# Rotary attention: two queue positions moved, ScalarE's half-precision copy of the queries and GpSimd's subtraction for it

## The chip, the cores and the metric

The program runs on one core of one Trainium2 chip. A core has five engines that run their own instruction queues and wait for each other by semaphores: TensorE (PE in the profile, PEld its weight loads), VectorE (DVE), ScalarE (ACT), GpSimd (POOL) and SyncE (SP, which issues transfers). The metric is the time of one execution on the device in microseconds; lower is better. Before the change it is 3782.42 us (median of 3 runs, 3779.88 to 3782.56).

## The reference

The whole network has eight parts in two layers (modulation, Nystrom attention, LSTM, head-routed attention; then adapter, rotary attention, recurrent network, experts). The change touches the rotary attention of the second layer alone:

```python
q = apply_rope(q)            # t*cos + rotate_half(t)*sin
k = apply_rope(k)
k = concatenate([pm, k]); v = concatenate([pm, v])     # 4 memory rows ahead of 512 tokens
scores = einsum('bhid,bhjd->bhij', q, k) * dim_head**-0.5
scores = where(causal, scores, finfo.min)
attn = softmax(scores, axis=-1)
out = einsum('bhij,bhjd->bhid', attn, v)
return out.transpose(...) @ w_out.T
```

It runs over 8 batches of 512 tokens with 16 heads of 64. Operands are kept in two half-precision parts, a high one (the value rounded) and a low one (what the rounding left), and TensorE multiplies high by high, high by low and low by high.

## The kernel before

`attention_core` takes the heads in pairs: 8 pairs in a batch, 2 batches in a turn of the loop, so 64 slots of one pair each, with a short run-in. A slot `s` works on four pairs at once: it ends pair `s-1` (weights times values, outputs), does the scores and the exponentials of pair `s`, the plain scores and maxima of pair `s+1`, and the projection and rotation of queries and keys of pair `s+2`. Each engine has its own function `rope_slot`, which is the order of its queue written out by hand. After every 8 pairs an output projection is added ("out" slots, L1028), and once in 8 slots the tokens of a later batch are split into high and low (`low_tokens`, L1151; called a new-batch slot here).

The rotation of one 128x512 block of queries (index `q`) or keys (index `k`) goes through four engines:

- PE projects into the PSUM tile `pj` (L832).
- DVE multiplies it by the cosines (L979) and shuffles neighbours (L980) into the two halves of `ab`, which releases `pj`.
- POOL multiplies the second half by the signed sines (`turn`, L1138) and adds the halves into `rot` (`sum_up`, L1142).
- ACT copies `rot` to half precision (`high`, L1080); POOL subtracts that from `rot` and stores the low part (`low`, L1147).

`ab` and `rot` are single buffers here. So DVE's next rotation waits for the sum before it, and a sum waits for `low` of the block before it.

The other DVE work named below: L1007 subtracts the high from the full exponentials, in four pieces for four key tiles of 128x1024, 776, 520 and 264 elements (called piece 0 to 3), with a tail of 4x8 (L1010); L990 and L991 are maxima of scores; L997, L1001 and L1003 split the maxima; L1024 makes the low part of the outputs; L1019 to L1021 normalise; L1014 makes the low values. On ACT L1088 and L1093 are the two exponentials of a tile (`exps`), L1101 keeps outputs, L1083 the turned maxima and L1098 the high values.

Of the kernel before, what the change touches and what calls it, by code (L numbers as in the profile page):

```python
# [760 lines left out]
def attention_core(nc, XT, HT, c_):  # L761
# [15 lines left out]
    def slots(run,eng):  # L777

        for s in (-2,-1,0): run(0,s)
        with loop(nc,eng,NB//BPI) as it:  # L780
            for s in range(1,S+1): run(it,s)
    def first_query(t): return max(0,P*t-PM) if rope else 0
    def key_columns(qt): return P*qt+P+PM if rope else T
    def written(t): return P_AT[t]+(PAD if rope and t else 0)
# [3 lines left out]
    with ExitStack() as ctx:  # L788
# [22 lines left out]
        def sliced(X,k,it): return X[:,k,bass.ds(it,1),:].rearrange("p a t -> p (a t)")  # L811
        block=ctx.enter_context(nc.Block())
        def batch(it,n): return (it*BPI+n//NP_)%NB
        def h_of(n): return hT[:,(n//NP_)%HB]
        def rot_of(j): return rot[:,0 if rope else j%2]
# [256 lines left out]
        @block.scalar  # L1072
        def _(act):
            act.wait_ge(cleared,CL)
            def high(it,j):
                n,what=divmod(j,2)
                if what and rope: nc.scalar.activation(QK[:,n%4,1,:,0:PM],c_.pmk[:,n%NP_],ACT.Copy).then_inc(pm_kept,1)
                act.wait_ge(summed if rope else evac,it*2*S+j+1)
                dst=QK[:,n%4,1,0,PM:PM+T] if what else QK[:,n%4,0,0,0:T]
                nc.scalar.activation(dst,rot_of(j),ACT.Copy).then_inc(hi,1)  # L1080
            def keep_max(it,n):
                act.wait_ge(m_turned,it*S+n+1)
                nc.scalar.activation(mT[:,:],mtp[:,0:T],ACT.Copy).then_inc(m_copied,1)  # L1083
            def exps(it,n,t):
                act.wait_ge(st_done,it*S*QT+n*QT+t+1)
                if n: act.wait_ge(pv_done,it*S*QT+(n-1)*QT+t+1)
                w_=T-first_query(t); at=written(t)
                nc.scalar.activation(PH[:,:,at:at+w_],st_ps[:,:,0:w_],ACT.Exp,scale=DH**-0.5)  # L1088
                if rope and t==QT-1:
                    a2=written(QT)  # L1090
                    nc.scalar.activation(PH[0:PM,:,a2:a2+PM],st_ps[0:PM,:,w_:w_+PM],ACT.Exp,scale=DH**-0.5)
                if n or t>1: act.wait_ge(p_low,it*S*QT+n*QT+t-1)
                i=nc.scalar.activation(P32[:,t%2,:,0:w_],st_ps[:,:,0:w_],ACT.Exp,scale=DH**-0.5)  # L1093
                if rope and t==QT-1: i=nc.scalar.activation(P32[0:PM,t%2,:,w_:w_+PM],st_ps[0:PM,:,w_:w_+PM],ACT.Exp,scale=DH**-0.5)
                i.then_inc(exped,1)
            def high_values(it,n):
                act.wait_ge(v_done,it*S+n+1)
                nc.scalar.activation(V[:,n%4,0:QT,0,:,0:DH],vo[:,:].rearrange("p (t h d) -> p t h d",t=QT,h=2),ACT.Copy).then_inc(v_hi,1)  # L1098
            def keep_outputs(it,n):
                act.wait_ge(o_turned,it*S+n+1)  # L1100
                if rope: nc.scalar.activation(ao[:,n%NP_,0,:],vo[:,:],ACT.Copy).then_inc(o_kept,1)  # L1101
                else: nc.scalar.activation(ao[:,n%NP_,:],vo[:,:],ACT.Identity,scale=c_.gate(batch(it,n),n%NP_),bias=c_.gated_bias(batch(it,n),n%NP_)).then_inc(o_kept,1)
            def high_tokens(it,n):
                if n>=NP_*HB: act.wait_ge(v_done,it*S+(n//NP_-HB+1)*NP_)
                for k in range(2):
                    nc.scalar.activation(h_of(n)[:,0,k,PM:PM+T],sliced(HT,k,batch(it,n)),ACT.Copy).then_inc(h_hi,1)
            def high_weights(it,n): c_.high_weights(act,it*BPI+n//NP_,n)
            def new_batch(s): return s+3>0 and (s+3)%NP_==0
            def rope_slot(it,s):
                if s>=1: exps(it,s-1,2); exps(it,s-1,3)  # L1110
                if s>=-1: high(it,2*(s+1)+1)
                if s>=0: keep_max(it,s)
                if new_batch(s): high_tokens(it,s+3)
                if s>=-1: high_values(it,s+1)
                if s>=0: exps(it,s,0)
                if s>=1: keep_outputs(it,s-1)
                if s>=0: exps(it,s,1)
                high(it,2*(s+2))
            def flat_slot(it,s):
                if s>=-1: high(it,2*(s+1))  # L1120
                if new_batch(s): high_tokens(it,s+3)
                if s>=1: exps(it,s-1,2)
                if new_batch(s): high_weights(it,s+3)
                if s>=-1: high_values(it,s+1)
                if s>=1: exps(it,s-1,3)
                if s>=0: keep_max(it,s)
                if s>=-1: high(it,2*(s+1)+1)
                if s>=0: exps(it,s,0)
                if s>=1: keep_outputs(it,s-1)
                if s>=0: exps(it,s,1)  # L1130
            high_tokens(0,0)
            if not rope: high_weights(0,0)
            slots(rope_slot if rope else flat_slot,act)
        @block.gpsimd
        def _(pool):
            def turn(it,j):
                pool.wait_ge(evac,it*2*S+j+1)
                nc.gpsimd.tensor_tensor(ab[:,1],ab[:,1],c_.tab[:,1],ALU.mult).then_inc(turned,1)  # L1138
            def sum_up(it,j):
                if j: pool.wait_ge(lo,it*2*S+j)  # L1140
                pool.wait_ge(turned,it*2*S+j+1)
                nc.gpsimd.tensor_tensor(rot_of(j),ab[:,0],ab[:,1],ALU.add).then_inc(summed,1)  # L1142
            def low(it,j):
                n,what=divmod(j,2)
                pool.wait_ge(hi,it*2*S+j+1)
                dst=QK[:,n%4,what,:,PM:PM+T] if what else QK[:,n%4,0,:,0:T]
                nc.gpsimd.tensor_tensor(dst[:,1],rot_of(j),dst[:,0],ALU.subtract).then_inc(lo,1)  # L1147
            def low_tokens(it,n):
                for k in range(2):
                    pool.wait_ge(h_hi,2*(it*BPI+n//NP_)+k+1)  # L1150
                    nc.gpsimd.tensor_tensor(h_of(n)[:,1,k,PM:PM+T],sliced(HT,k,batch(it,n)),h_of(n)[:,0,k,PM:PM+T],ALU.subtract).then_inc(h_ready,1)  # L1151
            def low_weights(it,n): c_.low_weights(pool,it*BPI+n//NP_,n)
            def new_batch(s): return s+3>0 and (s+3)%NP_==0
            def rope_slot(it,s):
                q,k=2*(s+2),2*(s+2)+1
                if s>=-1: low(it,2*(s+1)+1)
                turn(it,q); sum_up(it,q)
                if new_batch(s): low_tokens(it,s+3)
                turn(it,k)
                low(it,q)  # L1160
                sum_up(it,k)
            def flat_slot(it,s):
                if s>=-1: low(it,2*(s+1)); low(it,2*(s+1)+1)
                if new_batch(s): low_tokens(it,s+3); low_weights(it,s+3)
            pool.wait_ge(cleared,CL)
            low_tokens(0,0)
            if not rope: low_weights(0,0)
            slots(rope_slot if rope else flat_slot,pool)
# [1098 lines left out]
```

## Time and profile before

| | us |
|---|---|
| median of 3 runs | 3782.42 |
| profiled execution | 3805.44 |
| its span | 3803.5 |
| PE busy | 3140.8 (83%) |
| DVE busy | 2247.7 (59%) |
| ACT busy | 1692.0 (44%) |
| POOL busy | 1216.8 (32%) |

The profiled execution took 23.0 us more than the median of the timed ones. The rotary attention's slots fill 2097 us to 3018 us of the span. Over that stretch the granted clock of TensorE is 1.00, its full 2.4 GHz, and DVE is busy for 803.81 of 921.19 us and PE for 847.40. A busy share says little there, since the two engines alternate in who is late. The slots are alike to a few hundredths of a microsecond, so a single slot, read instruction by instruction, tells of most of them.

### The profile page before, as it was taken

The numbers are of one execution on the slowest core, as the hardware profiler recorded it, in microseconds if no ns is written. First come the engines' busy times: TensorE is split into PE (matmuls) and PEld (weight loads), VectorE is DVE, ScalarE is ACT, GpSimd is POOL, SyncE is SP. The second block draws the span as 40 slices with busy tenths as digits, with TensorE's granted clock in tenths as the row PEclk, the third lists the DMA queues.
The fourth block names the chain that finished last, engine by engine and source line by source line (L and its number), as shares of the span: only waits on it lengthen the run. The fifth ranks groups of instructions, "written<-read, shape, count | busy, mean of one in ns | idle before, by whom it ended". The sixth has DMA issues, their size and how long they took to land. (4 is left out here: it accounts for less than half of the span.)

```text
span 3803.5 us, 143700 instructions
## 1 busy us (share of the span) xinstructions
PE 3140.8 (83%) x58958; PEld 2400.2 (63%) x58958; DVE 2247.7 (59%) x6777; ACT 1692.0 (44%) x5164; POOL 1216.8 (32%) x1533
## 2 busy tenths in 40 slices
PE   8677488988889889689985899999999889999571
PEld 5545278888888888545532666666666567777451
DVE  4667644444444444478865888889888745555233
ACT  2179333333333333366743555556555534444230
POOL 0032410000000000133311655566555544443342
PEclk9899755555555555599997999999999955555786
DMA  4011110000000000011001000000000010110335
GB/s 133 1 55 46 31 26 14 14 25 14 25 14 14 25 14 25 15 33 25 17 1 52 2 2 3 2 3 3 2 3 2 16 51 30 32 33 28 109 102 173
DMA packets 110725, 116.07 MB, mean 31 GB/s; under 512 B 52782, under 2 KB 94199, under 8 KB 110112
## 3 DMA queue, kind: packets, MB, share of 16 engines
q1 hardware_dynamic: 102416, 87.33, 8.1%
q0 software_dynamic: 7824, 21.46, 1.6%
q8 instruction: 403, 6.60, 0.7%
q14 instruction: 82, 0.67, 0.1%
HBM read 79.62 MB, written 29.13 MB: 29 GB/s over the span
## 5 line engine op out<-in xcount | busy, mean ns | idle before, releaser
L676 PE MATMUL banks<-hp,whp 128*128 128x8 f16 x24576 | 741.6, 168 | 117.5 <-DVE hp L743 117.5
L676 PEld LDWEIGHTS banks<-hp,whp 128*128 128x128 f16 x24576 | 698.0, 104 | 178.2 <-DVE hp L743 169.4
L709 ACT ACTIVATE ig<-banks 128x32 f32<-128x32 f32 x512 | 100.9, 197 | 577.2 <-PE banks L676 577.2
L738 DVE SCALAR_TENSOR_TENSOR carry<-ig 128x16 f32<-128x16 f32 x512 | 91.6, 179 | 424.9 <-ACT ig L709 424.9
L646 POOL COPY HT<-hist 128x128 f32 x64 | 21.2, 407 | 986.6 <-DVE hp L748 986.6
L1088 ACT ACTIVATE att_PH<-att_stp 128x1024 f16<-128x1024 f32 (+3 forms) x258 | 183.2, 710 | 325.4 <-PE att_stp L888 325.4
L1753 PE MATMUL rnn_banks<-rnn_hp,rnn_whp 128*128 128x8 f16 x6144 | 285.4, 171 | 40.3 <-ACT rnn_hp L1811 15.4
L1753 PEld LDWEIGHTS rnn_banks<-rnn_hp,rnn_whp 128*128 128x128 f16 x6144 | 248.3, 107 | 107.1 <-ACT rnn_hp L1811 76.1
L1007 DVE TENSOR_TENSOR att_PL<-att_P,att_PH 128x1024 f16<-128x1024 f32 (+3 forms) x257 | 266.3, 1075 | 0.5 <-issue 0.2
L654 PE MATMUL banks<-xs,wxp 128*128 128x64 f16 x3168 | 263.7, 241 | 0.0
L1147 POOL TENSOR_TENSOR att_QK<-att_rot,att_QK 128x512 f16<-128x512 f32 x133 | 174.2, 1310 | 239.6 <-ACT att_QK L1080 239.6
L1905 DVE TENSOR_TENSOR rnn_hp<-rnn_hist,rnn_hp 128x16 f16<-128x16 f32 x512 | 97.7, 191 | 227.6 <-ACT rnn_hist L1812 218.7
L1811 ACT ACTIVATE rnn_hp<-rnn_banks 128x16 f16<-128x16 f32 x512 | 93.7, 183 | 279.5 <-PE rnn_banks L1753 277.4
L832 PE MATMUL att_pj<-att_hT,att_w 128*128 128x512 f16 x804 | 201.0, 386 | 17.4 <-POOL att_hT L1151 15.6
L990 DVE TENSOR_REDUCE att_mx<-att_sp 128x2 f32<-128x264 f32 (+3 forms) x263 | 209.6, 818 | 1.1 <-PE att_sp L862 1.1
L1138 POOL TENSOR_TENSOR att_ab<-att_ab,att_rope 128x512 f32<-128x512 f32 x134 | 169.8, 1267 | 124.2 <-DVE att_ab L980 123.4
L1142 POOL TENSOR_TENSOR att_rot<-att_ab 128x512 f32<-128x512 f32 x134 | 204.2, 1524 | 14.8
L654 PEld LDWEIGHTS banks<-xs,wxp 128*128 128x128 f16 x3168 | 194.5, 126 | 0.0
L1093 ACT ACTIVATE att_P<-att_stp 128x1024 f32<-128x1024 f32 (+3 forms) x258 | 180.6, 700 | 5.3 <-DVE att_PL L1007 5.3
L901 PE MATMUL att_acc<-att_V,att_PH 128*128 128x65 f16 (+1 forms) x3584 | 180.0, 193 | 0.0
L743 DVE TENSOR_TENSOR hp<-og,tc 128x16 f16<-128x16 f32 x512 | 90.1, 176 | 144.2 <-ACT tc L715 144.2
L901 PE MATMUL att_acc<-att_V,att_PL 128*128 128x65 f16 x1792 | 175.0, 192 | 0.0
(606 smaller groups left out, 7712.9 us busy)
## 6 DMA issues: line engine op xcount, KB each, us to landing
gen_w<-in_L_cond_W_dram SPq DMA_DIRECT2D x32, 512.0 KB
exp_xt<-expert_rows_scratch SPq DMA_DIRECT2D x80, 129.0 KB
edge_cb<-cols_scratch SPq DMA_DIRECT2D x16, 512.0 KB, 3.8
XT<-expert_found_scratch SPq DMA_DIRECT2D x16, 512.0 KB, 4.9
mod_xn<-in_x_dram SPq DMA_DIRECT2D x8, 512.0 KB
XT<-in_xT_dram SPq DMA_DIRECT2D x1, 4096.0 KB
out_dram<-exp_ob SPq DMA_DIRECT2D x64, 64.0 KB, 2.2
attw_st<-in_L_attn_w_qkvT_dram SPq DMA_DIRECT2D x6, 512.0 KB
```

The source lines that it names most:

```text
L654: last=nc.tensor.matmul(out, wxp[:,wpart,k,col:col+128], xs[:,st,xpart,k,steps], start=False,stop=False,skip_group_check=True)
L676: last=nc.tensor.matmul(out, whp[:,wpart,k,col:col+128], hp[:,k,hpart], start=False,stop=True,skip_group_check=True)
L832: last=nc.tensor.matmul(pj[:,:],c_.w_of(n)[:,wpart,k,col:col+P],h_of(n)[:,xpart,k,PM:PM+T],start=(i==0),stop=(i==5)); i+=1
L901: last=nc.tensor.matmul(out[:,0:wide],p[:,h,at:at+P],V[:,n%4,tt,part,h,0:wide],start=(tt==0 and a==0 and p is PH and part==0),stop=(tt==(R ...
L990: i=nc.vector.tensor_reduce(out=mx[:,:,qt:qt+1],in_=s_ps[:,:,at:at+w_],axis=X_AX,op=ALU.max); at+=w_
L1007: i=nc.vector.tensor_tensor(PL[:,:,at:at+w_],P32[:,t%2,:,0:w_],PH[:,:,at:at+w_],ALU.subtract)
L1088: nc.scalar.activation(PH[:,:,at:at+w_],st_ps[:,:,0:w_],ACT.Exp,scale=DH**-0.5)
L1093: i=nc.scalar.activation(P32[:,t%2,:,0:w_],st_ps[:,:,0:w_],ACT.Exp,scale=DH**-0.5)
L1138: nc.gpsimd.tensor_tensor(ab[:,1],ab[:,1],c_.tab[:,1],ALU.mult).then_inc(turned,1)
L1142: nc.gpsimd.tensor_tensor(rot_of(j),ab[:,0],ab[:,1],ALU.add).then_inc(summed,1)
L1147: nc.gpsimd.tensor_tensor(dst[:,1],rot_of(j),dst[:,0],ALU.subtract).then_inc(lo,1)
L1753: last=nc.tensor.matmul(pre(st,par)[:,u,j], whp[:,wpart,k,u*P:u*P+P], hp[:,k,hpart], start=False,stop=True,skip_group_check=True)
```

## The change

On ACT `high` of the queries of pair `s+2` moves from the end of the slot to a place between the exponentials of tile 0 and the copy of the outputs. On POOL `low` of the same queries moves from behind the keys' sine product (`turn(k)`) to a place ahead of it. Nothing is added or removed, and the operands of every instruction are the same.

```diff
@@ scalar, rope_slot
                 if s>=0: exps(it,s,0)
+                high(it,2*(s+2))
                 if s>=1: keep_outputs(it,s-1)
                 if s>=0: exps(it,s,1)
-                high(it,2*(s+2))
@@ gpsimd, rope_slot
                 turn(it,q); sum_up(it,q)
                 if new_batch(s): low_tokens(it,s+3)
+                low(it,q)
                 turn(it,k)
-                low(it,q)
                 sum_up(it,k)
```

ACT's queue in a steady slot, before (L1085 and L1078 are counters' arithmetic):

```order
L1088 ACTIVATE att_PH<-att_stp 128x2x512
L1093 ACTIVATE att_P<-att_stp 128x2x512
L1101 ACTIVATE att_ao<-att_vo 128x512
L1085 REGISTER_ALU
L1088 ACTIVATE att_PH<-att_stp 128x2x388
L1093 ACTIVATE att_P<-att_stp 128x2x388
L1078 REGISTER_ALU
L1080 ACTIVATE att_QK<-att_rot 128x512
```

The same place after the change:

```order
L1088 ACTIVATE att_PH<-att_stp 128x2x512
L1093 ACTIVATE att_P<-att_stp 128x2x512
L1078 REGISTER_ALU
L1080 ACTIVATE att_QK<-att_rot 128x512
L1101 ACTIVATE att_ao<-att_vo 128x512
L1085 REGISTER_ALU
L1088 ACTIVATE att_PH<-att_stp 128x2x388
L1093 ACTIVATE att_P<-att_stp 128x2x388
```

The copy L1080 has moved ahead of one 128x512 copy and of the two 128x776 exponentials.

POOL's queue over one slot, before (turn and sum of the queries, turn of the keys, low of the queries, sum of the keys, low of the keys):

```order
L1138 TENSOR_TENSOR att_ab<-att_ab,att_rope 128x512
L1142 TENSOR_TENSOR att_rot<-att_ab 128x512
L1138 TENSOR_TENSOR att_ab<-att_ab,att_rope 128x512
L1147 TENSOR_TENSOR att_QK<-att_rot,att_QK 128x512
L1142 TENSOR_TENSOR att_rot<-att_ab 128x512
L1147 TENSOR_TENSOR att_QK<-att_rot,att_QK 128x512
```

The same stretch after the change:

```order
L1138 TENSOR_TENSOR att_ab<-att_ab,att_rope 128x512
L1142 TENSOR_TENSOR att_rot<-att_ab 128x512
L1147 TENSOR_TENSOR att_QK<-att_rot,att_QK 128x512
L1138 TENSOR_TENSOR att_ab<-att_ab,att_rope 128x512
L1142 TENSOR_TENSOR att_rot<-att_ab 128x512
L1147 TENSOR_TENSOR att_QK<-att_rot,att_QK 128x512
```

The first L1147 and the second L1138 have changed places; the queues of PE, DVE and SP are the same as before.

## Rows read from the trace of the kernel before

**Rows 1.** Waits, 2109 to 3018 us: total us, times, longest us.
```profile
ACT att_PH L1088 <- PE att_stp L888: 325.4, 249, 9.7
```

**Rows 2.** Windows of an ordinary and a new-batch slot: busy time by engine.
```profile
2378.83:2391.73 12.90, 11.93 (x215) 8.45 (x215) 12.23 (x24) 8.13 (x18) 8.17 (x7) 1.00 0.01 1
2404.64:2417.72 13.08, 11.93 (x215) 8.46 (x215) 12.54 (x24) 8.31 (x18) 9.05 (x7) 1.00 0.01 3
```

**Rows 3.** Timeline of DVE, the ordinary slot: start us, us, line, [idle <-releaser].
```profile
2378.67 0.16 DVE L991 TENSOR_REDUCE att_mx<-att_sp 128x2 f32<-128x8 f32 x1
2379.34 1.21 DVE L1007 TENSOR_TENSOR att_PL<-att_P,att_PH 128x1024 f16<-128x1024 f32 x1
2380.47 1.92 DVE L1007 TENSOR_TENSOR att_PL<-att_P,att_PH 128x776 f16<-128x776 f32 x1
...
2385.05 0.15 DVE L1010 TENSOR_TENSOR att_PL<-att_P,att_PH 4x8 f16<-4x8 f32 x1
...
2386.76 0.21 DVE L1019 RECIPROCAL att_inv<-att_acc 128x8 f32<-128x8 f32 x1 [0.29 <-PE att_acc L901]
...
2389.47 0.69 DVE L979 TENSOR_TENSOR att_ab<-att_pj,att_rope 128x512 f32<-128x512 f32 x1 [0.23 <-PE att_pj L832]
```

**Rows 4.** Timeline of POOL, the same slot.
```profile
2375.04 1.27 POOL L1142 TENSOR_TENSOR att_rot<-att_ab 128x512 f32<-128x512 f32 x1
...
2380.22 1.35 POOL L1147 TENSOR_TENSOR att_QK<-att_rot,att_QK 128x512 f16<-128x512 f32 x1 [0.97 <-ACT att_QK L1080]
2381.65 1.87 POOL L1142 TENSOR_TENSOR att_rot<-att_ab 128x512 f32<-128x512 f32 x1
2385.36 1.16 POOL L1147 TENSOR_TENSOR att_QK<-att_rot,att_QK 128x512 f16<-128x512 f32 x1 [1.84 <-ACT att_QK L1080]
```

**Rows 5.** Timeline of ACT, the same slot.
```profile
2375.80 1.02 ACT L1093 ACTIVATE att_P<-att_stp 128x1024 f32<-128x1024 f32 x1
2377.00 0.60 ACT L1101 ACTIVATE att_ao<-att_vo 128x512 f16<-128x512 f32 x1 [0.18 <-PE att_vo L906]
...
2378.81 0.81 ACT L1093 ACTIVATE att_P<-att_stp 128x776 f32<-128x776 f32 x1
2379.51 0.63 ACT L1080 ACTIVATE att_QK<-att_rot 128x512 f16<-128x512 f32 x1
```

**Rows 6.** Timeline of ACT in the run-in, a copy that waits for POOL.
```profile
2114.03 0.63 ACT L1080 ACTIVATE att_QK<-att_rot 128x512 f16<-128x512 f32 x1 [0.27 <-POOL att_rot L1142]
```

**Rows 7.** Timeline of POOL in the run-in, what that copy waited for.
```profile
2112.13 1.86 POOL L1142 TENSOR_TENSOR att_rot<-att_ab 128x512 f32<-128x512 f32 x1
```

**Rows 8.** Timeline of DVE, the new-batch slot.
```profile
2405.16 1.52 DVE L1007 TENSOR_TENSOR att_PL<-att_P,att_PH 128x1024 f16<-128x1024 f32 x1
...
2411.17 0.15 DVE L1010 TENSOR_TENSOR att_PL<-att_P,att_PH 4x8 f16<-4x8 f32 x1
```

**Rows 9.** Timeline of POOL, the new-batch slot.
```profile
2400.87 1.27 POOL L1142 TENSOR_TENSOR att_rot<-att_ab 128x512 f32<-128x512 f32 x1
...
2404.33 1.27 POOL L1138 TENSOR_TENSOR att_ab<-att_ab,att_rope 128x512 f32<-128x512 f32 x1
...
2411.18 1.18 POOL L1147 TENSOR_TENSOR att_QK<-att_rot,att_QK 128x512 f16<-128x512 f32 x1 [1.53 <-ACT att_QK L1080]
...
2414.07 1.27 POOL L1142 TENSOR_TENSOR att_rot<-att_ab 128x512 f32<-128x512 f32 x1
```

**Rows 10.** Timeline of DVE in two out slots.
```profile
2226.74 0.96 DVE L1007 TENSOR_TENSOR att_PL<-att_P,att_PH 128x776 f16<-128x776 f32 x1
...
2229.38 1.70 DVE L1007 TENSOR_TENSOR att_PL<-att_P,att_PH 128x520 f16<-128x520 f32 x1
...
2344.51 1.10 DVE L1003 SCALAR_TENSOR_TENSOR att_mparts<-att_mx,att_mparts 128x8 bf16<-128x8 f32 x1
```

**Rows 11.** Timeline of POOL in the same out slots.
```profile
2229.37 1.16 POOL L1147 TENSOR_TENSOR att_QK<-att_rot,att_QK 128x512 f16<-128x512 f32 x1 [11.89 <-ACT att_QK L1080]
...
2344.40 1.16 POOL L1147 TENSOR_TENSOR att_QK<-att_rot,att_QK 128x512 f16<-128x512 f32 x1 [11.98 <-ACT att_QK L1080]
```

## The prediction

> **What bounds the kernel now.** I looked first at the page's slices and then at the waits of the stretch that the change touches. ACT waits 325.4 us there for PE [rows 1], so moving a ScalarE copy saves nothing by itself. The question is what the move sets off on POOL and, through it, on DVE. Next come the windows of single slots: an ordinary one takes 12.90 us, with DVE busy for 12.23 and PE for 11.93 [rows 2]. Then the timelines of one slot. All times below are counted from the end of L991 in that slot (2378.83), written as +t. DVE has two short gaps: 0.29 us before L1019 and 0.23 us before L979, both ended by PE [rows 3]. So PE sets the 12.9 us by a hair. DVE has 0.29 us to spare between L991 and L1019, and a delay beyond that lengthens the slot.
>
> The second thing to see is that DVE and POOL hold each other off. Piece 1 of the subtraction (128x776) takes 1.92 us in the ordinary slot [rows 3] and 0.96 us where POOL is idle [rows 10]. It ends 0.82 us after L1147 does (2381.57, 2382.39), as if it had begun only then, and the L1142 that started at 2381.65 ends 1.13 us after piece 1 does, taking 1.87 where it takes 1.27 elsewhere [rows 3, 4]. One waits for the whole instruction of the other. It concerns DVE's instructions with two inputs in SBUF (L1007, L1010, L1003).
>
> The Trainium skill, "SBUF — State Buffer", "SBUF: two separate sides", says that a DVE instruction with two SBUF inputs and a GpSimd instruction take a shared port pair as an exclusive lock, whoever starts first. The trace agrees with the 1.92 against 0.96; what it adds is who is next when both wait, below.
>
> **Who is next.** The earlier start goes first, down to 0.01 us. L1147 at 2380.22 goes ahead of piece 1 at 2380.47 while piece 0 still runs [rows 3, 4]. In an out slot L1147 at 2229.37 makes piece 2 at 2229.38 take 1.70 [rows 10, 11]. In the new-batch slot L1010 at 2411.17 keeps its 0.15 against L1147 at 2411.18 [rows 8, 9]. Even a tiny DVE instruction pays in full: L1003 takes 1.10 behind L1147 (2344.40 and 2344.51) [rows 10, 11].
>
> **The change part by part.** Nothing is added, so each instruction keeps its own length, and the cost lies in what meets what.
>
> ACT: `high(q)` starts once the exponential of tile 0 ends (2376.82) less the 0.11 by which such a copy starts early (2379.51 against 2379.62) [rows 5], at -2.12; its input, POOL's sum, is there at 2376.31 [rows 4]. Queued behind it are L1101 and the exponentials of tile 1. L1101 would start at -2.12+0.63-0.11 = -1.6 instead of -1.83 (2377.00) and end at -1.0, ahead of its reader on DVE, which comes behind L991. The second exponential of tile 1 starts at -0.02 (2378.81) [rows 5], which leaves a microsecond for the first. So ACT costs 0; if that cover failed, PE would wait the tenths by which they slip, at most 0.2 in a slot, 0.2x56 = 11 us.
>
> POOL: from the start of `high(q)` it is 0.63 copy, 0.08 to wake POOL, 1.16 `low(q)`, 0.02, and 1.27 `turn(k)`, 3.16 in all. `turn(k)` thus ends at +1.04, where before POOL was free again at 2379.25 (2380.22 less its idle 0.97 [rows 4]), +0.42. Piece 0 starts at +0.51 [rows 3] and is held. The new-batch slot shows what that costs: `turn(k)` ends at 2405.60 and piece 0 at 2406.68, 1.08 later [rows 8, 9]. `sum_up(k)` is queued by then and goes next, ending 1.13 after piece 0; piece 1 ends 0.82 after that. From its end to L1010 is 2.66 (2382.39 to 2385.05) [rows 3]. So L1010 starts 3.16+1.08+1.13+0.82+2.66 = 8.85 after `high(q)`: at +6.73 instead of +6.22.
>
> What L1010 meets there is the keys' `low`, L1147, which hangs on PE and ACT and comes at +6.53 (2385.36) [rows 4]. Before, L1010 was ahead of it, by 0.31 in the ordinary slot. If L1010 comes second, it waits for piece 3 to end (0.08 after its own start), for L1147 (1.02 more, as 2381.57 less piece 0's end 2380.55), and ends 0.05 later, 1.15 instead of 0.15: a cost of 1.0 us. The slot's length, when DVE sets it, is L1010's start plus 6.55 (2411.17 to 2417.72) [rows 2, 8].
>
> **The sum by slots.** The length of one slot sets `high(q)` of the next. Two limits: the exponentials, at -2.12 less the amount by which the slot before exceeded 12.91; and POOL's sum, which in a slot set by DVE ends at -2.38 (2415.34 against 2417.72) [rows 9], plus 0.03 (2113.99 to 2114.03, rounded) [rows 6, 7]: -2.35.
>
> - Type A, behind an out slot or a long slot: `high(q)` at -2.35, L1010 at +6.50, just ahead of L1147. Length 6.50+6.55 = 13.05.
> - Type C, behind type A: -2.12-0.14 = -2.26, L1010 at +6.59, behind L1147 by 0.06. Length 6.59+6.55+1.0 = 14.14.
>   In such a slot PE also waits, for piece 3 and its tail, but only at its last weights-times-values, some 0.5 us, while DVE's delay is 1.3; so DVE still sets the end, and the next exponentials come early enough for POOL's sum to be the limit: type A again.
> - New batch: `low(q)` now comes 2.19 behind POOL's sum (as `turn(k)` did, 2402.14 to 2404.33) [rows 9], -0.19 to +0.97. The same chain gives 0.97+1.08+1.13+0.82+2.66 = 6.66, behind L1147: 14.21.
> - Out slots: DVE waits some 10 us for PE ahead of piece 0, and POOL is through. No change.
>
> Between two out slots there are seven: A C A C new-batch A C, 3x13.05+3x14.14+14.21 = 95.8 us, against 6x12.91+13.08 = 90.5. That is +5.2, and for eight such groups +42; I take 41, since the run-in and one late slot in two groups are different already. The profiled execution would go from 3805.4 to 3846.4. The timed runs lie 23.0 us below the profiled one before, and I keep that: 3782.4+41 = 3823 us, +1.1%.
>
> **Why it can hardly gain.** PE's path through the slot is not touched. If DVE's stalls all went, the ordinary slot would stay at 12.91; only the eight new-batch slots could drop, 8x0.17 = 1.4 us, and a few tenths in out slots.
>
> **Rivals.**
> 1. L1010 is not held although it comes 0.06 second, for instance because DVE keeps the ports from piece 3 on. For it: no row of before has L1010 behind L1147; against it: L1003, which is as small, was held. Then C is 6.59+6.55 = 13.14 and the new batch 13.21: 91.8 against 90.5 in a group, 8x1.2 = +10, 3792 us. Chance 0.19.
> 2. L1010 of type A is late too (its lead is 0.03 by my sum, and the terms are good to 0.02 each). Each of 24 A slots costs 1.0 more: +65, 3848 us. Chance 0.10.
> 3. The other side: taking `low(q)` from under piece 1 frees DVE. Piece 1 drops from 1.92 to 0.96 and POOL pays instead. It decides at one point: `sum_up(k)` would have to start after piece 1 does. Against it: a held piece 0 ends 1.08 after `turn(k)`, so `sum_up(k)` is asked for most of a microsecond ahead of piece 1. As PE sets the slot, it would save only the 1.4 us and few tenths reckoned above: 3781, not slower. Chance 0.05.
> 4. The moves cancel: `high(q)` comes later than I reckon or POOL's chain is shorter, L1010 is ahead of L1147 everywhere and DVE's 0.29 swallows most of it: 3785. Chance 0.06.
>
> The forecast has 0.60.
>
> **How the numbers follow.** About 0.2% (7.6 us) is what can be told from no change. The forecast (0.60) and rival 2 (0.10) are slower. Rival 1 is slower by 10 us, so about a fifth of its 0.19 falls inside 7.6. Rivals 3 and 4 lie inside but for 0.03, which I leave for faster. That makes faster 0.03, within 0.12, slower 0.85. The range is 3785 to 3850: its low end takes in rival 1 and the edge of rival 4, its high end rival 2. The forecast's own range is 3808 to 3836, by whether one A in four is late or one C in three is early.
>
> **What would show it.** L1147 of the queries starts 0.71 behind its copy, at -1.64 or -1.55, instead of at +1.39. Piece 0 goes from 1.21 to 1.38 in type A and 1.47 in type C (+0.51 to +1.89 or +1.98). Piece 1 is held by `sum_up(k)` instead of `low(q)` and takes about 2.04. L1010 takes 1.15 in half of the slots: its 64 instances sum to some 42 us instead of 64x0.15 = 9.6. Slots alternate between 13.05 and 14.14. PE gains idle time before the last weights-times-values (L901), some 0.5 us in a long slot. If L1010 stays at 0.15 everywhere, rival 1 or 4 is true; if piece 1 falls to 1.0, rival 3. Nothing outside 2090 to 3030 us may change.

## The result, and the profile after

| | before | after |
|---|---|---|
| timed runs, median (lowest to highest) | 3781.15 (3779.59 to 3782.56, 4 runs) | 3826.45 us (3817.79 to 3831.33, 4 runs) |
| profiled execution / its span | 3805.44 / 3803.5 | 3826.23 / 3824.3 |
| mean granted clock | 0.745 | 0.747 |

The ratio is 1.0117, 95% interval 1.0098 to 1.0136: slower by 45.3 us, where 41 were forecast.

The two profiled executions are only 20.8 us apart, and the windows show why. The first row is before, the second after, each for the recurrence that follows the attention, up to its last L1905. The columns are those of [rows 2]: stretch, its length, busy time of PE, PEld, DVE, ACT and POOL with their instructions, granted clock, DMA share, GB/s.

```profile
3045.00:3513.00 468.00, 425.82 (x7839) 358.87 (x7839) 235.16 (x1387) 192.73 (x1259) 209.19 (x517) 0.50 0.11 35
```
```profile
3092.00:3554.00 462.00, 424.05 (x7855) 356.62 (x7852) 240.33 (x1388) 193.17 (x1262) 209.87 (x519) 0.50 0.12 36
```

The execution profiled of before spent 468 us here and 185 in the expert products. That of after spent 461 and 166, and the profiles of the experiments below are like it (457 to 461 and 164 to 166). The change doesn't touch these stages; before's profile had drawn an execution that was some 27 us longer there. In the slots of the attention (2097.19 to 3018.38 before, 2099.62 to 3066.22 after) it is 921.2 us before and 966.6 after, +45.4, the whole timed difference.

Windows of after, first a pair of slots that alternate as forecast, then three in a row. The second of these three was forecast short, and the third is a surprise of another kind, with a granted clock of 0.88:

```profile
2377.71:2391.82 14.11, 12.11 (x215) 8.51 (x215) 13.44 (x25) 8.57 (x18) 8.29 (x7) 1.00 0.01 2
2391.82:2404.81 12.99, 11.93 (x215) 8.45 (x215) 12.45 (x25) 7.50 (x17) 8.00 (x7) 1.00 0.01 1
...
2258.28:2272.40 14.12, 12.11 (x215) 8.50 (x215) 13.45 (x24) 8.57 (x18) 8.30 (x7) 1.00 0.01 3
2272.40:2286.57 14.17, 12.11 (x215) 8.51 (x215) 13.27 (x24) 8.03 (x17) 8.21 (x7) 1.00 0.01 3
2286.57:2301.05 14.48, 13.50 (x215) 9.21 (x215) 12.62 (x25) 8.47 (x19) 9.03 (x8) 0.88 0.01 1
```

PE's own work is 11.93 in the short slot, as in [rows 2], and 12.11 in the long one; DVE's grows from 12.23 before to 12.45 and 13.44. The timeline of DVE shows where: piece 0 and the tail, first in the long slot (counted from 2377.71), then in the short one (from 2391.82).

```profile
2378.22 1.46 DVE L1007 TENSOR_TENSOR att_PL<-att_P,att_PH 128x1024 f16<-128x1024 f32 x1
2384.28 1.14 DVE L1010 TENSOR_TENSOR att_PL<-att_P,att_PH 4x8 f16<-4x8 f32 x1
...
2392.34 1.30 DVE L1007 TENSOR_TENSOR att_PL<-att_P,att_PH 128x1024 f16<-128x1024 f32 x1
2398.24 0.15 DVE L1010 TENSOR_TENSOR att_PL<-att_P,att_PH 4x8 f16<-4x8 f32 x1
```

POOL over the same two slots:

```profile
2384.25 1.16 POOL L1147 TENSOR_TENSOR att_QK<-att_rot,att_QK 128x512 f16<-128x512 f32 x1 [3.44 <-ACT att_QK L1080]
...
2390.18 1.16 POOL L1147 TENSOR_TENSOR att_QK<-att_rot,att_QK 128x512 f16<-128x512 f32 x1 [0.74 <-ACT att_QK L1080]
2391.29 1.27 POOL L1138 TENSOR_TENSOR att_ab<-att_ab,att_rope 128x512 f32<-128x512 f32 x1
2392.70 2.07 POOL L1142 TENSOR_TENSOR att_rot<-att_ab 128x512 f32<-128x512 f32 x1
...
2398.36 1.17 POOL L1147 TENSOR_TENSOR att_QK<-att_rot,att_QK 128x512 f16<-128x512 f32 x1 [3.59 <-ACT att_QK L1080]
```

The keys' L1147 comes 0.03 ahead of the tail in the long slot and 0.12 behind it in the short one. That 0.15 of a microsecond decides whether a 4x8 subtraction takes 0.15 or 1.14. In a long slot TensorE waits for the tail, here at 2385:

```profile
2385.48 0.23 PE L901 MATMUL att_acc<-att_V,att_PH 128*128 128x65 f16 x2 [0.41 <-DVE att_PL L1010]
```

That wait of 0.41 doesn't set the slot's length. DVE's own queue does, which runs through GpSimd: behind the tail DVE prepares the next rotation (L979, L980), GpSimd multiplies and sums it, and only then can DVE go on, 0.53 late and no longer held up by TensorE:

```profile
2389.56 0.69 DVE L979 TENSOR_TENSOR att_ab<-att_pj,att_rope 128x512 f32<-128x512 f32 x1 [0.53 <-POOL att_rot L1142]
```

The groups of DVE over after's attention (from 2109 to 3040 us, so 62 or 63 of the 64 pairs), and L901 from the page:

```profile
L1007 DVE TENSOR_TENSOR att_PL<-att_P,att_PH 128x776 f16<-128x776 f32 x62 | 118.2, 1907 | 0.5 <-issue 0.2
L1007 DVE TENSOR_TENSOR att_PL<-att_P,att_PH 128x1024 f16<-128x1024 f32 x63 | 87.3, 1385 | 0.0
L1010 DVE TENSOR_TENSOR att_PL<-att_P,att_PH 4x8 f16<-4x8 f32 x62 | 33.6, 542 | 0.0
...
L901 PE MATMUL att_acc<-att_V,att_PH 128*128 128x65 f16 (+1 forms) x3584 | 183.6, 193 | 12.0 <-DVE att_PL L1010 11.9
```

Over the 64 pairs the tail takes 34.9 us, where it was 9.4 before and 42 were forecast; 26 of the 64 are held, where 32 were forecast.

### The profile page after: what moved, and what is told of

Same layout as the page of the kernel before. It is cut to its first block and busy times, and to the rows that moved or that the text cites. A ratio compares the mean times of both kernels' runs of the same rounds, so it can differ in the third digit from the quotient of the medians.

```text
span 3824.3 us, 143700 instructions
## 1 busy us (share of the span) xinstructions
PE 3154.1 (82%) x58958; PEld 2404.7 (63%) x58958; DVE 2289.8 (60%) x6777; ACT 1685.3 (44%) x5164; POOL 1210.6 (32%) x1533
## 5 line engine op out<-in xcount | busy, mean ns | idle before, releaser
L1007 DVE TENSOR_TENSOR att_PL<-att_P,att_PH 128x1024 f16<-128x1024 f32 (+3 forms) x257 | 279.1, 1122 | 8.2 <-ACT att_P L1094 7.7
L1147 POOL TENSOR_TENSOR att_QK<-att_rot,att_QK 128x512 f16<-128x512 f32 x133 | 154.8, 1164 | 340.2 <-ACT att_QK L1080 340.2
L1905 DVE TENSOR_TENSOR rnn_hp<-rnn_hist,rnn_hp 128x16 f16<-128x16 f32 x512 | 99.3, 194 | 215.6 <-ACT rnn_hist L1812 203.9
L1142 POOL TENSOR_TENSOR att_rot<-att_ab 128x512 f32<-128x512 f32 x134 | 212.7, 1587 | 19.6 <-POOL att_ab L1138 1.0
L832 PE MATMUL att_pj<-att_hT,att_w 128*128 128x512 f16 x804 | 203.5, 390 | 17.2 <-POOL att_hT L1151 15.4
L1138 POOL TENSOR_TENSOR att_ab<-att_ab,att_rope 128x512 f32<-128x512 f32 x134 | 177.9, 1328 | 67.1 <-DVE att_ab L980 67.0
L901 PE MATMUL att_acc<-att_V,att_PH 128*128 128x65 f16 (+1 forms) x3584 | 183.6, 193 | 12.0 <-DVE att_PL L1010 11.9
L901 PEld LDWEIGHTS att_acc<-att_V,att_PH 128*128 128x128 f16 x3584 | 168.3, 97 | 17.9 <-DVE att_PL L1010 12.6
L901 PE MATMUL att_acc<-att_V,att_PL 128*128 128x65 f16 x1792 | 177.6, 192 | 0.0
```

The source lines that it names most:

```text
L832: last=nc.tensor.matmul(pj[:,:],c_.w_of(n)[:,wpart,k,col:col+P],h_of(n)[:,xpart,k,PM:PM+T],start=(i==0),stop=(i==5)); i+=1
L901: last=nc.tensor.matmul(out[:,0:wide],p[:,h,at:at+P],V[:,n%4,tt,part,h,0:wide],start=(tt==0 and a==0 and p is PH and part==0),stop=(tt==(R ...
L1007: i=nc.vector.tensor_tensor(PL[:,:,at:at+w_],P32[:,t%2,:,0:w_],PH[:,:,at:at+w_],ALU.subtract)
```

## The experiments

Each ratio is against the kernel before on the same chip (3778.0 us for experiments 1 to 4, 3780.37 for 5 to 7). The changed kernel was timed against 3781.15, so what an experiment gives back of its loss is told by the ratios and by the time of the attention in the profiles.

**1. The ScalarE move alone.**

```
-                high(it,2*(s+2))        # in the slot's ACT list, late
+                high(it,2*(s+2))        # behind tile 0's exponentials
 (POOL's list as in before: turn(k), then low(q))
```

> ScalarE's copy is moved as in the change, GpSimd's queue is that of before (turn of the keys, then low of the queries). Theory (DVE and POOL hold each other off, and the earlier start goes first): low(q) is ready when turn(k) ends at +0.42, so it starts at +0.43, 0.08 ahead of piece 0 (+0.51). Piece 0 is held to +2.67, sum_up(k) goes next to +3.80, piece 1 ends at +4.62, and low(k) (+6.53) now meets piece 2 and holds piece 3. Every ordinary slot is about 14.8 us, some 3890 us in all, more than the whole change costs. Rival (an early copy on ScalarE costs nothing by itself, the cost comes from GpSimd's new order): 3781 us.

Measured: 3871.47 us (3870.98 to 3874.8) against 3778.0, ratio 1.0246, 1.0231 to 1.0262. Most slots take 14.74, near the 14.8 expected. The total was expected 19 us too high, since not every slot is of this kind: the out slots stay as they were, but for one with a lower clock, five of the new-batch slots take 14.15 to 14.17, and eleven slots take 14.4 to 14.5 with a lower clock. This is DVE over its attention:

```profile
L1007 DVE TENSOR_TENSOR att_PL<-att_P,att_PH 128x1024 f16<-128x1024 f32 x61 | 118.6, 1944 | 0.0
L1007 DVE TENSOR_TENSOR att_PL<-att_P,att_PH 128x776 f16<-128x776 f32 x61 | 115.2, 1889 | 0.5 <-issue 0.2
L1007 DVE TENSOR_TENSOR att_PL<-att_P,att_PH 128x264 f16<-128x264 f32 x60 | 63.2, 1053 | 5.5 <-ACT att_P L1094 5.5
```

Piece 0 (1.21 in [rows 3]) is held for most of a GpSimd product, and piece 3 (0.42 free) too. Moving ScalarE's copy alone is worse than the whole change, since `low(q)` then lands right ahead of piece 0.

**2. The GpSimd move alone.**

```
-                turn(it,k)              # ahead of low(q)
                 low(it,q)
+                turn(it,k)              # behind low(q)
 (ACT's list as in before)
```

> GpSimd's queue is moved as in the change, ScalarE's is that of before, so low(q) waits for the copy until +1.23 and turn(k) waits behind it. Theory: low(q) holds piece 1 as before; turn(k) is asked for at +2.76 and ends at +4.70, sum_up(k) runs from behind L997 to +6.02 and holds L1003 (asked at +5.15), which takes about 0.9 instead of 0.20; then low(k) holds the 4x8 tail as well. Slots of 14.4 to 14.5 us, some 3870 us. Rival (the wait for the copy is hidden, GpSimd has 4 us of idle time in a slot): within 10 us of 3781.

Measured: 3884.16 us (3880.8 to 3886.54) against 3778.0, ratio 1.0277, 1.0261 to 1.0292; slots of 14.77. The size was expected too small, and the place was wrong: L1003 (0.29 on average) and the tail (0.23) are held in only 6 and 5 of the 64 pairs. Held in most are L1001 and piece 3:

```profile
L1007 DVE TENSOR_TENSOR att_PL<-att_P,att_PH 128x264 f16<-128x264 f32 x60 | 67.2, 1120 | 3.2 <-ACT att_P L1094 3.2
L1001 DVE TENSOR_SCALAR att_mparts<-att_mx 128x8 bf16<-128x8 f32 x60 | 60.8, 1013 | 2.0
```

One of those L1001 on DVE's timeline, and the GpSimd sum that it waits out on POOL's:

```profile
2384.51 1.22 DVE L1001 TENSOR_SCALAR att_mparts<-att_mx 128x8 bf16<-128x8 f32 x1
```
```profile
2384.41 1.27 POOL L1142 TENSOR_TENSOR att_rot<-att_ab 128x512 f32<-128x512 f32 x1
```

L1001 has one input in SBUF, not two, and takes 0.19 elsewhere. Of its 60 instances here 51 began while a GpSimd product ran, and 48 of these were held; the other three began within 0.01 us of the product. My class of held instructions was too narrow (last section).

**3. The tail issued ahead of piece 3, on top of the change.** This takes the 4x8 subtraction out of the place where it meets the keys' `low`; the same instructions run.

```
-                i=tensor_tensor(PL[..piece..])
-                if rope and t==QT-1: i=tensor_tensor(PL[..tail..])
-                i.then_inc(p_low,1)
+                if rope and t==QT-1: tensor_tensor(PL[..tail..])
+                tensor_tensor(PL[..piece..]).then_inc(p_low,1)
```

> The changed kernel, with the 4x8 tail of the subtraction (L1010) issued ahead of piece 3 instead of behind it: the last DVE instruction with two SBUF inputs then starts 0.27 us earlier, at +6.3 in a long slot, ahead of low(k) at +6.53. Theory: the 1.0 us of the long slots goes, they fall from 14.11 to about 13.14, the drops of TensorE's granted clock go too, and the time is 3792 us, +0.3% on before. Rival (the long slots come from pieces 0 and 1 being held longer, the tail only shows the wait): 3815 us or more.

Measured: 3784.48 us (3781.26 to 3786.72, 11 runs) against 3778.0 (21 runs), ratio 1.0015, 1.0006 to 1.0024. Behind the run-in the slots between the out slots take 12.96 to 12.99, 13.11 to 13.15 and, for the new batch and a slot with a late L1003 (see below), 13.19 to 13.27. Line L1009 is the tail here; one of its 64 is still held, in an out slot:

```profile
L1009 DVE TENSOR_TENSOR att_PL<-att_P,att_PH 4x8 f16<-4x8 f32 x64 | 10.4, 163 | 0.0
```

The change alone costs 1.17%, with this swap 0.15%; the attention falls from 966.6 to 929.1 us, where before has 921.2. So the order of two instructions gives back 37 of the 45 us: 25 in the 26 long slots, 9 in six slots and 3 in two out slots of after that had a lower TensorE clock (see below), of which this profile has none. What is left is the later chain behind piece 0 (13.14 instead of 12.91 in a long slot), as reckoned.

**4. The keys' `low` 0.2 us later, on top of the change.** Two more small copies on ScalarE ahead of the copy that it waits for; work is added, none removed.

```
                 if what and rope:
+                    activation(spare[:,n%2,0],c_.pmk[:,n%NP_],ACT.Copy)
+                    activation(spare[:,n%2,1],c_.pmk[:,n%NP_],ACT.Copy)
                     activation(QK[:,n%4,1,:,0:PM],c_.pmk[:,n%NP_],ACT.Copy)
```

> The changed kernel, with two more copies of 128x8 (about 0.1 us each) on ScalarE ahead of its copy of the keys, into a spare tile: low(k) starts 0.2 us later, at +6.73. Theory: L1010 of a long slot starts at +6.58, now ahead of low(k), keeps its 0.15 us, and the long slots fall to about 13.15 although work was added; 3792 us. Rival (who goes first is not settled by who starts first): still 3826 us or more.

Measured: 3785.97 us (3784.12 to 3793.04, 11 runs) against 3778.0, ratio 1.002, 1.0011 to 1.0029; the attention takes 931.1 us. No tail is held (L1011 here):

```profile
L1011 DVE TENSOR_TENSOR att_PL<-att_P,att_PH 4x8 f16<-4x8 f32 x64 | 9.4, 148 | 0.0
```

Adding 132 instructions to the slower kernel makes it 1% faster. Experiment 3 moved the tail and this one moved L1147, and each took away nearly all of the loss: the meeting of the two is what costs. Both also rid the kernel of most of the lower clock, which one slot in this profile has (14.51 us at 0.88, behind an out slot).

**5. The same with one added copy**, to find the edge.

> As the run with two extra copies, with one: low(k) starts at +6.63. L1010 of an ordinary long slot (+6.58) is ahead by 0.05, that of a new-batch slot (+6.64) and of the four slots with a late L1003 (+6.67) are behind by 0.01 to 0.04. Theory: ordinary slots all near 13.1, up to 12 slots of 64 still long: 3792 to 3806 us. Rival (a wider window than 0.05 us decides): 3826 us.

Measured: 3796.8 us (3792.11 to 3798.38) against 3780.37, ratio 1.0044, 1.0029 to 1.006. Six tails are held (15.4 us over all 64): four in slots with a late L1003 and two of the new batch, the slots in which the tail comes latest (+6.65 to +6.70). The order of starts held to 0.01 us, as the theory had it. Two slots have the lower clock (14.49 and 14.47). The tail's group:

```profile
L1011 DVE TENSOR_TENSOR att_PL<-att_P,att_PH 4x8 f16<-4x8 f32 x64 | 15.4, 241 | 0.0
```

**6. The tail first, in the kernel before (control).** The edit of experiment 3 on before.

> The kernel before with the 4x8 tail ahead of piece 3. There the tail was never held in an ordinary slot, so this control should change nothing: 3781 us within 0.1%. If the new order of the two subtractions gained by itself, it would show here.

Measured: 3782.69 us (3777.95 to 3786.76, 11 runs) against 3780.37, ratio 1.0001, 0.999 to 1.0012; its attention takes 921.4 us, as before's 921.2. So the order of the tail is worth nothing by itself, and what experiment 3 gives back comes from its no longer being held.

**7. Longer slots without a held instruction.** Two more 128x512 products with an input in PSUM in the queries' rotation of before (`rotate`, into a spare tile), to see whether slots of 14 us bring a lower TensorE clock by themselves.

```
                     if what==0:
+                        tensor_tensor(spare[:,n%2,0],pj[:,:],c_.tab[:,0],ALU.mult)
+                        tensor_tensor(spare[:,n%2,1],pj[:,:],c_.tab[:,0],ALU.mult)
```

> The kernel before with two more products of 128x512 on VectorE in the rotation of the queries (0.61 us each, one operand in PSUM, so not held by GpSimd), into a spare tile: each ordinary slot becomes 12.77+1.22 = 13.99 us with no instruction held longer. Theory on the third kind of slot seen after the change (14.48 us at a granted clock of 0.88 behind two or three long slots): it comes from TensorE's idle time in long slots, so it shows here too, and the time is above 3781+1.08x64 = 3850 us. Rival (it comes with the held instructions): clock 1.00 throughout and 3848 to 3850 us.

Measured: 3894.08 us (3889.97 to 3901.85) against 3780.37, ratio 1.0297, 1.0281 to 1.0312. Of the 56 slots between the out slots 20 take 13.97, as reckoned. In 32 the clock is lower (0.89) and they take 15.2 to 15.5, and four of the new batch take 15.35 at full clock with a held tail, which was not expected. The window from 2300 to 3100 us has a mean granted clock of 0.95, where before's attention has 1.00:

```profile
2300.00:3100.00 800.00, 694.03 (x10849) 461.29 (x10847) 672.26 (x1243) 409.82 (x803) 447.73 (x310) 0.95 0.01 2
```

But for those four tails the held instructions of DVE are as many as in before, and none of the 32 slots with the lower clock has a held tail. So the clock can fall without further held instructions, in a kernel whose TensorE is less busy (694 of 800 us, where before's has 847 of 921). That idle time is the cause is argued, not shown: experiment 7 changed the slots' length and their rhythm as well, and even in the profiles of experiments 4 and 5, whose slots are mostly as short as 13.0 to 13.2, the clock fell in one slot (14.51) and in two (14.49 and 14.47).

## Why the prediction was right, and where it was off

- **Who goes next.** Right, and the time hangs on it: tail behind L1147 by 0.03, held; ahead by 0.12, free. Rival 1 (a tail that comes 0.06 second is not held) falls with the row of 1.14; experiment 3 shows what it would have been, 6 us instead of 45. Rival 2 (type A held too) was 0.12 away. Rival 3 falls with piece 1's 1.91 on average (2.03 in most slots, 2.04 forecast); its cost to `sum_up(k)` is the 2.07 above. TensorE's wait ahead of L901, forecast at 0.5 in a long slot, is 11.9 us over 26, 0.46 each.
- **A and C alternate.** Right in two of the eight groups as a whole (the first and the third) and at the start of five more. Type C was forecast at 14.14 with the tail at +6.59 and is 14.11 with +6.57. The new batch was forecast at 14.21 and is 14.14 to 14.17 in five groups; in the other three it comes behind a slot with a lower clock, its tail is free and it takes 13.06 to 13.09.
- **A slot that was read too lightly.** In the second, fourth and sixth group the alternation breaks at the third slot, at full clock. This slot was forecast short, but its L1003 starts 0.23 later than in the others, so that the tail comes at +6.66 and is held. The slot at 2272.40:

```profile
2277.99 0.20 DVE L1003 SCALAR_TENSOR_TENSOR att_mparts<-att_mx,att_mparts 128x8 bf16<-128x8 f32 x1 [0.27 <-DVE att_mparts L1001]
2279.06 1.12 DVE L1010 TENSOR_TENSOR att_PL<-att_P,att_PH 4x8 f16<-4x8 f32 x1
```

  Before has the same late L1003 in four groups (slots of 13.01 to 13.05 with the tail at +6.46 to +6.48). The prediction counted it in two, and took 1 us off its sum for it and the run-in, though it adds held tails. It makes two long slots in a row, and in all three groups the next slot is one with a lower clock.
- **Type A**, forecast at 13.05, is 12.98. The mis-sized term is the 0.02 between `low(q)` and `turn(k)`: L1138 at 2391.29 starts 0.05 before L1147's record ends (2391.34), so `turn(k)` ends at +0.74 instead of +0.81, piece 0 takes 1.30 and not 1.38, and the tail comes at +6.42. In type C most of this gain is lost again, since `high(q)` comes at -2.20 and not -2.26.
- **A step that was missing: TensorE's clock.** Six slots take 14.46 to 14.48 with a granted clock of 0.88 (a part of them at 1.2 instead of 2.4 GHz), and two out slots 25.92 with 0.93. L838's and L832's matmuls of the slot at 2286 take 1.61 and 2.12 instead of 1.18 and 1.47, the keys' `low` comes at +8.10, and so no tail is held there: DVE waits for ScalarE's exponential instead. These eight slots are 12.6 us longer than before's, more than a quarter of the whole loss, and the prediction had no term for it. The six held tails that it had too many, 1.0 us each, stood for half of it.

```profile
2294.00 0.43 DVE L1007 TENSOR_TENSOR att_PL<-att_P,att_PH 128x264 f16<-128x264 f32 x1 [1.28 <-ACT att_P L1094]
2294.35 0.15 DVE L1010 TENSOR_TENSOR att_PL<-att_P,att_PH 4x8 f16<-4x8 f32 x1
```

  Of the 56 slots between the out slots, 24 are short (as forecast), 26 long with a held tail, and 6 slow by the clock, where 32 held tails were forecast. The 24 is a coincidence: 17 of these stand where a short slot was forecast, and 22 of the 26 long ones where a long one was.
- **The sum.** These 56 slots take 766.7 us, and 724.7 before: +42, where +42 was forecast. That this agrees so well is partly luck: only 39 of the 56 are of the kind forecast for their place, the short ones take 13.01 on average and were forecast 0.04 too long, and the six with the lower clock are 0.3 longer than the long slot that was forecast for three of them and 1.4 longer than the short one that was forecast for the other three. The out slots, forecast unchanged, add 3.3, nearly all of it in the two with the lower clock. With 0.1 in the run-in it is the 45.4 of the attention.
- **Profile and median.** I took the distance of 23.0 us between before's profiled and timed runs as lasting. It wasn't: after's profiled execution lies on its median, 3826 and not the 3846 that was forecast for it. The forecast of the timed runs doesn't suffer, since it is their median before plus the difference of the slots.

## What to carry to other kernels

On two engines that exclude each other, add up the start times, not the busy times: ask for each instruction of the class what of the other engine is asked for just ahead of it. The shortest one can pay as much as the longest (here 0.99 for the 4x8 tail and 1.07 for piece 1), so put it where the other engine is idle, or ahead of a long one of its own. When two instructions meet within a tenth of a microsecond, test the edge from both sides (here a swap of two instructions, and a delay by added copies) before keeping or dropping the whole idea. Here neither test beat the kernel before: they show what the loss was, and the change itself gains nothing.

## What the runs showed of the hardware that was not expected

- **One input is enough.** L1001, a TENSOR_SCALAR of 128x8 from SBUF to SBUF, is held like the others: 1.22 where it takes 0.19. L997 (two inputs of 128x2) was held once in after, 1.17 instead of 0.16. Every instruction that was seen held has all its inputs in SBUF; L1014, L1021 and L1024, with one in PSUM, started beside GpSimd products in nearly every slot (L1024 not in experiment 2) and kept their 0.67 to 0.69. The Trainium skill, "SBUF — State Buffer", "Who interferes with whom", has this: `tensor_scalar` can enter a mode that takes both ports. The trace agrees by the held L1001 of experiment 2, 52 over all 64 pairs, and the prediction, which spoke of two inputs only, had missed it; it cost experiment 2's expectation, not the forecast.
- **The edge is sharp.** In the profiles of before, after and experiments 4 and 5 tail and L1147 meet within 0.6 us 224 times. The tail was free (0.15) whenever it started up to 0.013 us behind L1147, 192 times, and held (1.12 to 1.16) from 0.014 on, 32 times, with no exception. Experiments 1, 2 and 7 have no exception either. In the four profiles a held tail ends 1.17 to 1.27 after L1147 starts.
- **A slower clock without a stop.** TensorE's granted clock fell from 2.4 to 1.2 GHz 1.6 to 1.9 us into a slot, five times in after behind two long slots in a row, in each of which TensorE was busy for 12.1 of 14.1 us, and once behind an out slot; in two out slots it fell 0.5 us in, behind one long slot. In three groups two long slots in a row were not followed by it. In experiment 7 the mean is 0.95, and no idle stretch of TensorE in the attention is longer than 2.3 us. The Trainium skill, "TensorE: Matmul & The Clock Gate", Part 1, says that the throttled state is the default and activity releases it. The runs can't confirm that; they show the lower level in the midst of work. What it is in the idle stretches that tips the clock stays open.
